# The third direction's combining product in stored order, with a transposed second add

## The reference

```
xs_h = x.transpose(2, 0, 1, 3)
ctx_above = _direction(xs_h, ...d).transpose(1, 2, 0, 3)
ctx_below = _direction(xs_h[::-1], ...u)[::-1].transpose(1, 2, 0, 3)
xs_w = x.transpose(3, 0, 1, 2)
ctx_left = _direction(xs_w[::-1], ...r)[::-1].transpose(1, 2, 3, 0)
ctx_right = jnp.zeros_like(ctx_left)
context_map = jnp.concatenate([ctx_above, ctx_below, ctx_left, ctx_right], axis=1)
out = jnp.einsum('bchw,oc->bohw', context_map, w_comb) + b_comb[None, :, None, None]
...
x = x + _L0_conv_ref(_gn(x), ...)
```

## Time and profile before

| what | value |
|---|---|
| time, median of 3 runs (lowest to highest) | 404.64 us (403.96 to 406.71) |
| span of the profiled execution, first to last instruction | 401.3 us |
| median of the runs less that span | 3.3 us |
| TensorE busy | 360.2 us, 90% |
| VectorE busy | 296.8 us, 74% |
| ScalarE busy | 275.4 us, 69% |
| mean granted TensorE clock | 0.967 of full speed |

### The profile page before, as it was taken

How to read it: one execution, slowest core, us unless ns; L and a number is a source line. 1 busy time by engine, 2 the same in 40 slices (tenths; PEclk the granted TensorE clock), 3 DMA queues, 4 the chain that set the end, 5 groups by cost and what they waited for, 6 DMA issues and landing times.

```text
span 401.3 us, 7957 instructions
## 1 busy us (share of the span) xinstructions
PE 360.2 (90%) x2702; PEld 262.5 (65%) x2702; DVE 296.8 (74%) x750; ACT 275.4 (69%) x573; POOL 15.9 (4%) x26
## 2 busy tenths in 40 slices
PE   0105789999999999999999999999999999999996
PEld 0002668888888888888888888888888861222221
DVE  0659989899898898998998998998988982212111
ACT  6538878888878888888788788888888869000000
POOL 1074010000000000000000000000000000000000
PEclk9999999999999999999999999999999997689688
DMA  8700000000000000000000000000000001111112
GB/s 311 304 0 1 1 2 2 0 0 0 0 0 0 0 0 0 0 0 0 0 0 0 0 0 0 0 0 0 0 0 0 0 0 54 70 61 52 53 52 78
DMA packets 4183, 10.43 MB, mean 26 GB/s; under 512 B 593, under 2 KB 721, under 8 KB 4177
## 3 DMA queue, kind: packets, MB, share of 16 engines
q1 hardware_dynamic: 4176, 10.36, 6.7%
HBM read 6.16 MB, written 4.19 MB: 26 GB/s over the span
## 4 chain that ended last, share of the span: by engine, by line
PE 84%; ACT 6%; DVE 4%; issue 2%; POOL 2%; DMA 1%; SPq 0%; ACTq 0%; POOLq 0%
PE rz_bank L683 19%; PE conv_bank L683 15%; PE rz_bank L686 10%; PE n_bank L683 10%; PE conv_bank L686 7%; PE n_bank L686 5%; PE n_bank L776 3%; PE n_bank L774 3%; PE rz_bank L772 3%; PE n_bank L772 3%; PE rz_bank L776 3%; PE rz_bank L774 3%; DMA ctx_store<-weights_dram 1%; ACT rz L405 1%; ACT ctx_store L340 1%
## 5 line engine op out<-in xcount | busy, mean ns | idle before, releaser
L683 PE MATMUL conv_bank<-ctx_store,w_parts 128*128 (+1 forms) x558 | 108.9, 275 | 2.6 <-ACT ctx_store L428 2.1
L683 PE MATMUL rz_bank<-h_parts,w_parts 128*128 128x256 f16 x372 | 76.2, 273 | 0.1
L405 ACT ACTIVATE rz<-rz_bank,descale 128x512 f32<-128x512 f32 x96 | 66.0, 688 | 7.6 <-PE rz_bank L683 2.4
L686 PE MATMUL conv_bank<-ctx_store,w_parts 128*128 (+1 forms) x279 | 67.2, 275 | 0.0
L683 PEld LDWEIGHTS conv_bank<-ctx_store,w_parts 128*128 128x128 f16 x558 | 54.2, 97 | 19.1 <-ACT ctx_store L428 8.4
L417 ACT ACTIVATE nval<-npre 128x256 f32<-128x256 f32 x93 | 38.5, 414 | 40.5 <-DVE npre L625 40.5
L613 DVE SCALAR_TENSOR_TENSOR npre<-n_bank,descale,rz 128x256 f32<-128x256 f32 x93 | 45.0, 484 | 24.4 <-ACT rz L405 24.2
L683 PE MATMUL rz_bank<-x_rows,w_parts 128*128 (+1 forms) x256 | 52.4, 273 | 1.9 <-issue 1.9
L422 ACT ACTIVATE hval<-conv_bank,biases,descale 128x256 f32<-128x256 f32 x93 | 52.2, 561 | 0.0
L683 PE MATMUL n_bank<-h_parts,w_parts 128*128 128x256 f16 x186 | 45.7, 273 | 0.0
L686 PE MATMUL rz_bank<-h_parts,w_parts 128*128 128x256 f16 x186 | 45.6, 273 | 0.0
(11 more groups left out here) (89 smaller groups left out, 526.5 us busy)
## 6 DMA issues: line engine op xcount, KB each, us to landing
x<-x_dram SPq DMA_DIRECT2D x8, 512.0 KB, 9.1
out_dram<-x_rows SPq DMA_DIRECT2D x16, 256.0 KB, 2.0
ctx_store<-weights_dram SPq DMA_DIRECT2D x3, 576.0 KB, 5.0
ctx_store<-weights_dram SPq DMA_DIRECT2D x1, 192.0 KB, 6.0
biases<-biases_dram SPq DMA_DIRECT2D x1, 2.0 KB, 11.4
```

Of the source, the lines that this page charges most:

```text
L405: nc.scalar.activation(rz[k][:].rearrange("p g c -> p (g c)"), rz_bank[k][:], ACT.Sigmoid, scale=gate_scale(k)).then_inc(sig_done[k], 1)
L683: last = nc.tensor.matmul(out, w_block(HI, k, n), parts(hi_or_lo), start=start, stop=stop and hi_or_lo == LO, skip_group_check=True)
L686: last = nc.tensor.matmul(out, w_block(LO, k, n), parts(HI), start=False, stop=False, skip_group_check=True)
```

## The change

Direction 2 of a chunk leaves the shared accumulation. `chunk_columns(c)` reads its context in the order in which it is stored (32 runs of 16 cells: for each image column the 16 rows of this chunk) and writes three products into a bank of its own, one of `y_col_bank = [conv_bank[0], conv_bank[1], rz_bank[2], n_bank[2]]`. That bank holds the pixels column by column. Directions 0 and 1 keep their six products in `y_bank`. VectorE first adds `y_bank` and the residual into `y_sb`, as before, and waits for that to be done (`y_rows_summed`). In a second pass over the same 512 elements it adds the column bank in place, reading it with rows and columns exchanged: its PSUM operand then has a step of 16 float32 (64 bytes) from element to element, and its other operand and the output are contiguous. `y_summed` comes from the second pass.

```
--- before.py
+++ after.py
@@ -124,6 +124,7 @@
         n_bank = [bank(f"n_bank_{k}") for k in range(DIRS)]
         conv_bank = [bank(f"conv_bank_{i}") for i in range(2)]
         y_bank = [rz_bank[0], n_bank[0], rz_bank[1], n_bank[1]]
+        y_col_bank = [conv_bank[0], conv_bank[1], rz_bank[2], n_bank[2]]
         avg_bank = [conv_bank[0], conv_bank[1], n_bank[2]]
 
 
@@ -170,6 +171,7 @@
         h_hi_done = per_dir("h_hi_done")
         h_lo_done = per_dir("h_lo_done")
         y_ready = sem("y_ready")
+        y_rows_summed = sem("y_rows_summed")
         x_biased = sem("x_biased")
         y_summed = sem("y_summed")
         y_stored = sem("y_stored")
@@ -664,7 +666,12 @@
                 dve.wait_ge(x_biased, c + 1)
                 nc.vector.scalar_tensor_tensor(y_sb[:, c, :], y_bank[c % RING][:],
                                                descale[:, 2 * DIRS:2 * DIRS + 1], residual(c),
-                                               ALU.mult, ALU.add).then_inc(y_summed, 1)
+                                               ALU.mult, ALU.add).then_inc(y_rows_summed, 1)
+                dve.wait_ge(y_rows_summed, c + 1)
+                y_rows = y_sb[:, c, :].rearrange("p (h w) -> p h w", h=CHUNK_ROWS)
+                nc.vector.scalar_tensor_tensor(
+                    y_rows, y_col_bank[c % RING][:].rearrange("p (w h) -> p h w", w=W),
+                    descale[:, 2 * DIRS:2 * DIRS + 1], y_rows, ALU.mult, ALU.add).then_inc(y_summed, 1)
 
         @block.tensor
         def _(pe):
@@ -764,9 +771,6 @@
                 out = y_bank[c % RING][:].rearrange("p (h w) -> p h w", h=CHUNK_ROWS)
 
                 def ctx_part(p):
-                    if k == 2:
-                        cells = slice(1 + part * CHUNK_ROWS, 1 + (part + 1) * CHUNK_ROWS)
-                        return ctx_store[2][:, p, :, b, cells].rearrange("p w h -> p h w")
                     return ctx_store[k][:, p, rows, b, 1:1 + LINE]
 
                 nc.tensor.matmul(out, w_parts[:, HI, k, :], ctx_part(HI), start=k == 0, stop=False,
@@ -774,7 +778,22 @@
                 nc.tensor.matmul(out, w_parts[:, LO, k, :], ctx_part(HI), start=False, stop=False,
                                  skip_group_check=True)
                 return nc.tensor.matmul(out, w_parts[:, HI, k, :], ctx_part(LO), start=False,
-                                        stop=k == DIRS - 1, skip_group_check=True)
+                                        stop=k == 1, skip_group_check=True)
+
+            def chunk_columns(c):
+
+                b, part = divmod(c, CHUNKS_B)
+                out = y_col_bank[c % RING][:].rearrange("p (w h) -> p w h", w=W)
+
+                def ctx_part(p):
+                    return ctx_store[2][:, p, :, b, 1 + part * CHUNK_ROWS:1 + (part + 1) * CHUNK_ROWS]
+
+                nc.tensor.matmul(out, w_parts[:, HI, 2, :], ctx_part(HI), start=True, stop=False,
+                                 skip_group_check=True)
+                nc.tensor.matmul(out, w_parts[:, LO, 2, :], ctx_part(HI), start=False, stop=False,
+                                 skip_group_check=True)
+                return nc.tensor.matmul(out, w_parts[:, HI, 2, :], ctx_part(LO), start=False, stop=True,
+                                        skip_group_check=True)
 
             def steps(t, j):
                 k, s = lagged(t, j, 2)
@@ -823,13 +842,13 @@
                 chunk_part(c, 1)
             pe.wait_ge(ctx_lo_done[2], STEPS)
             for c in range(RING):
-                chunk_part(c, 2).then_inc(y_ready, 1)
+                chunk_columns(c).then_inc(y_ready, 1)
             for c in range(RING, B * CHUNKS_B):
 
                 pe.wait_ge(y_summed, c - RING + 1)
-                for k in range(DIRS):
-                    last = chunk_part(c, k)
-                last.then_inc(y_ready, 1)
+                for k in range(DIRS - 1):
+                    chunk_part(c, k)
+                chunk_columns(c).then_inc(y_ready, 1)
 
 
 def _weight_sets():
```

## The result

The changed kernel takes 367.04 us (median of 4 runs, 366.35 to 368.09), the kernel before beside it 404.3 us (402.24 to 406.71). The ratio is 0.909, with a 95% interval of 0.905 to 0.913. In a second comparison it was 0.909 again (0.906 to 0.913). The forecast was 368.6 with a range of 366.5 to 373.5.

A forecast was written before the change was run, and what follows sets the result against it. The prediction took TensorE to bound the tail, slowed by direction 2's operand order and the low clock. Savings of 8.1 and 29.1 us, with VectorE's passes at the end, gave 36.0 off the span: 404.64 - 36.0 = 368.6 us, range 366.5 to 373.5.

The forecast's parts named there:

- The bound and the order of reading: Tail: TensorE is the bound, and direction 2 products cost 0.918 us against 0.230 because of their operand's reading order.
- the products don't get cheaper: Rival, direction 2 products: 16-cell runs go at the lone-element rate as before, time 405.8 us; chance 0.02.
- The price of a product: Direction 2 products: 32 runs of 16 cells add 0.024 us to 0.218, so 0.242 us each, between 0.230 and 0.262.
- The first four chunks: Start of the tail: twelve direction 2 products at 0.242 us run from 332.56 to 335.46, 8.1 us less.
- The twelve chunks: Rest of the tail: 2.106 us a chunk, 25.3 us in place of 54.34, so 29.1 us less.
- The clock: Tail: TensorE's clock stays full, since it fell only behind slow products; 4.8 us of the twelve chunks' saving.
- VectorE's second pass: Each tail chunk: the stepped PSUM read takes 1.13 us, with 0.75 as lower bound.
- Whether VectorE keeps up: Tail: VectorE needs 1.83 us a chunk, under TensorE's 2.106, so its passes lie beside the products except the last two.
- One sign: Changed kernel's profile, tail: VectorE waits for TensorE before each first pass, not the reverse.
- the second rival: VectorE becomes the bound if its second pass takes over 1.41 us; at 2.46 us the time is 390; chance 0.06.
- the slower one: Rival, VectorE's second pass: at 8 ns an element it takes 4.32 us, time 420 us; chance 0.01.
- The sum: Whole kernel: span 401.3 to 365.3 us, 36.0 less; with 3.3 us kept outside the span, 404.64 becomes 368.6.

The follow-up runs named there:

- run-length table: Changed kernel with direction 2's operand read in runs of 16, 8, 4 or 2 cells in different chunks; one run of 372.7 us.
- one execution with four slow chunks: Changed kernel with direction 2's products of chunks 0 to 3 in pixel order, the rest in stored order; one run of 376.5 us.
- exchange in SBUF: Changed kernel with VectorE's second pass reading the column bank contiguously and stepping through its SBUF operand and output instead; one run of 368.2 us.
- the third pass: Changed kernel with a dependent third VectorE pass per chunk adding zero times the column bank; 372.70 us, ratio 0.919 to the kernel before.

## Why the prediction was right

**The bound and the order of reading.** TensorE set the tail's end before and does after, and the order in which direction 2's operand is read was the whole of the difference. The own banks with the old order bring nothing (ratio 1.004), so it is not the banks. The rival "the products don't get cheaper" is out by the 0.2425 us of a product.

**The price of a product.** 0.242 us forecast from 16 and no breaks, 0.2425 measured. The first four chunks: 2.91 us against 2.90. The twelve chunks: 25.23 against 25.27. The run-length table shows that this straight line holds only down to runs of 8; with runs of 4 the same working would have come out 8% low, with 2 by 28%.

**The clock.** It stayed at 1.00, as taken from the scan. That slow products bring it down was only argued in the prediction; one execution with four slow chunks bears it out, since its clock fell 3.4 us after they began and the changed kernel's did not. What stays open is when it falls among mixed chunks: in the profile before, the clock was 1.00 again from 347 to 357 us, through the slow products of two whole chunks, and fell three times more before the products ended. Their share of 4.8 us in the twelve chunks was read rightly off one execution, but it differs from run to run: the spans of the ten runs with own banks and old order go from 402.7 to 408.1 as the mean clock goes from 0.971 to 0.950. The execution before, at 0.967, was near the middle of its kind.

**VectorE's second pass.** This term was mis-sized: 1.13 us was taken, 0.751 measured, the lower bound. I had carried the price of lone SBUF elements over to PSUM; the sentence "a lone element from each place is nearer to it than a pair" failed. In SBUF the price would have been right (1.12), in PSUM, at a step of 64 bytes, it is nothing. The term's error cost the forecast 0.4 us, since only the last chunk's pass is on the path. The Trainium skill, VectorE: DVE Perf Modes, Mode 1x (REGULAR), has one result per cycle whatever the step and with PSUM operands. The trace agrees for the PSUM side (751 ns against 748), and not for the SBUF side (1122).

**Whether VectorE keeps up.** It does, with 1.45 us a chunk where 1.83 was forecast. One sign was too strong: VectorE waits for TensorE before ten of its sixteen first passes, not before each, for in chunks 1 to 6 it is still catching up with the four chunks that became ready within 2.9 us. At 1.83 us a chunk (exchange in SBUF) it still keeps up; the third pass moves it to 2.17, and there it is the bound. The mechanism of the second rival and of the slower one is real, and its turning point lies between the two, where the forecast has TensorE's 2.1 us.

**The sum.** The span came out at 364.6 against 365.3: 0.4 of it the second pass, 0.24 the earlier start of the tail in this execution. The larger error was outside the span. I kept 3.3 us between span and time, but where both are on record the distance is 1.7 to 1.8 us (366.35 with 364.6 after, 405.43 with 403.7 before). If it was 1.7 in the execution profiled before too, that one took 403.0 us, 1.6 below the median that the saving was taken from; its own time is not on record, so this is worked out and not shown. So 368.6, less 0.7 for the span, less 1.6 for what lies outside it, plus 0.7 by which the median after lies above its profiled run, gives 367.0. That the last of these errors ran against the others is luck: the spans of the changed kernel's ten runs go from 364.6 to 367.0, so a forecast from one profile can't be right to better than 1 us or so but by chance.

## What to carry to other kernels

Read the distance from start to start of neighbouring products by the order of their operand, not by their shape: here the same 512 columns cost 0.23 or 0.92 us, and the slow ones take the clock down with them, which the others then pay for. When an exchange of rows and columns is needed somewhere, try it on each side: as TensorE's operand (a step of 544 bytes) it cost 0.68 us a product, as TensorE's output (128 bytes) 0.19, as VectorE's SBUF operand and output (128) 0.37 a pass, and as VectorE's PSUM operand (64) nothing. A second pass on an engine that is not the bound costs its own length once, at the end, and an earlier start of the first pass takes even that back.

## What the hardware showed that I had not expected

- VectorE reads PSUM with a step of 64 bytes as fast as without one (751 ns for 512 float32, 748 contiguous), while the same exchange in SBUF, with a step of 128 bytes, takes it 1122 ns.
- TensorE's output with a step of 128 bytes costs 0.43 us for 512 columns at 1.00, with the clock undisturbed: twelve products of 0.43 us in a row, and groups of three at 0.57 us between faster ones, left it at 1.00; those of 0.918 brought it to 0.50 after 3.4 to 5 us.
- A break in the operand costs about 0.8 ns down to runs of 8 cells of two bytes, and 1.4 ns for runs of 2 or 1; a run of 4 lies between (0.95 ns).
